# The gate products of a scan-and-feed-forward block are put into silu's pause, and two chunks' finish moves a slot ahead

## Chip, cores and metric

One core of one Trainium2 chip. The metric is the device time in microseconds, the median of several executions. Lower is better.

## What is computed

```python
h = layernorm(x) * (1 + ca) + sa                     # x: 2048 tokens x 256
delta = softplus(dt @ dt_proj_w + dt_proj_b)         # dt, B, C: parts of h @ x_proj_w
for each token t:                                    # 16 states n for each of the 256 channels
    s[n] = exp(delta_t * A[n]) * s[n] + delta_t * B_t[n] * h_t
    y_t  = sum_n C_t[n] * s[n] + D * h_t
x = x + ga * y
h = layernorm(x) * (1 + cb) + sb
x = x + gb * (((silu(h @ gate_w.T * gate_s)) * (h @ up_w.T * up_s)) @ down_w.T * down_s)   # 704 wide
```

## The kernel before

The 2048 tokens are four chunks of 512; the 256 channels are two halves of 128 partitions. The kernel runs in steps. Step c (0 to 3) scans chunk c, and a step has 16 slots, one for each state n. Beside the scan, step c does the front (names with F: first normalization, projections, softplus, `u`) of chunk c+1 and the feed-forward part (names with K) of chunk c-1, whose last tasks run over into step c+1. Step 4 is the tail: the feed-forward part of chunk 3, with nothing to scan.

In a slot n of a scanning step:

- ScalarE (ACT) makes `decay` for each half, an exp of 512 columns (line 830). The ring of decays has two buffers, so the decay of a scan can start only when the scan two before it has ended (line 829).
- GpSimd (POOL) makes the drive `u*B[n]` for both halves three slots ahead (line 642).
- VectorE (DVE) runs the two scans s n.0 and s n.1 (line 995).
- The product `C[n]*state` is made one slot later (`KEEP_LAG`), by POOL for the n in `POOL_C` (line 654), else by DVE (line 969). For DVE's, TensorE (PE) first spreads row n of C over the partitions into the one bank `rows_ps` (line 1294). This row matmul waits until the last DVE product has read the bank.
- PE adds each product into `sums` three slots later, by eight 128x128 transposes (line 1320); the last three of a chunk come together in slot 0 of the next step.

The side tasks stand in tables by hand, `PLAN` and its special cases, as (slot, task) for each engine; an engine runs its slots strictly in order. Slot 12 is after the first half's scan or decay, 12.5 after the second half's. Slots of 16 and over lie in the next step (17 is slot 1). The K tasks in order: `x2` (DVE, line 895, adds `sums` to the residual when all 16 adds are done), `st0 st1 agg` (statistics), `rstd` (ACT) and `nmr` (POOL, line 617), `xn0 xn1` (ACT, line 713), `h2T` (PE transposes), `hi0 hi1` (ACT, line 745) and `lo0 lo1` (DVE, line 933), `gate0..4` and `mixed` (PE products, line 1241, then an ACT eviction each, line 799), `up0..4` (PE), `silu` (ACT, line 818: an activation table load, the silu of the five gates in one instruction, the silu of the sixth, half gate, and a table load back), `hdn5` (line 942) and `hdn0..4` (line 953) on DVE, which multiply silu's result by the up products, `down0..3` (PE, lines 1273 and 1274, each a block of 128 tokens; they wait for hdn5 and hdn4), and `out0 out1` (DVE, line 960), each for two downs. PE has three side banks; `PLACE` gives each product its bank, and a product waits until the user before has emptied it. `rows_ps` and the two decay banks count as banks 3 to 5.

The front's tasks on the same engines include `xT` (PE), `hmod0 hmod1` (ACT, line 728), `z` (PE, line 1193), `abs`, `zb`, `exp`, `ln` (ACT), `bc` (PE, line 1193, and ACT), `clo` (DVE, line 901), `delta0 delta1` (DVE, line 909).

Chunk 0's downs and outs stand in `SPREAD`, chunk 1's in `LATER`, chunk 2's whole K part in `CLOSING`, chunk 3's in `FINAL`. The end of the scanning is thus: last scan of step 3, product 15, its add, `x2` of chunk 3, then the tail.

Of the kernel before, what the change touches and what calls it, by code (L numbers as in the profile page):

```python
# [43 lines left out]
POOL_C = [[4, 6, 9, 11, 13]] + [[1, 3, 5, 7, 9, 11, 13]] * (NCH - 3) + [[1, 3, 5, 6, 7, 10, 13]] + [[1, 2, 4, 5, 7, 8, 10, 12, 13, 14]]  # L44
# [39 lines left out]
SECOND_LATER = {"st0": -7, "st1": -7, "agg": -7}  # L84
# [27 lines left out]
        (19, "K out0"), (22, "K out1"),  # L112
# [1280 lines left out]
```

## Time and profile before

| what | us |
|---|---|
| median of three runs | 315.76 (315.1 to 317.17) |
| the profiled execution, its own time | 314.61 |
| its span in the trace | 312.8 |
| DVE busy in the span | 256.8 (82%) |
| PE busy | 248.9 (80%) |
| POOL busy | 227.0 (73%) |
| ACT busy | 183.7 (59%) |

The span is the time from the first to the last instruction in the trace; the execution's own time lies 1.81 us above it. Matmul time is modelled in part, so a busy PE is not a PE at its peak. The mean granted TensorE clock was 0.874 of the full one.

### The profile page before, as it was taken

Reading aid. Unit: us, or ns where it says so; the run is one execution under the profiler, and the core shown is the slowest. Engines: PE = TensorE matmul, PEld = TensorE weight load, DVE = VectorE, ACT = ScalarE, POOL = GpSimd, SP = SyncE. Lnnn points to the kernel's source line nnn. Section 1 sums busy time; section 2 is a strip of 40 time slices with the busy share of each in tenths; the row PEclk is TensorE's granted clock in tenths of the full one; section 3 lists DMA queues with packets and bytes.
Section 4 is the critical chain, followed back from the end, with each engine's and each line's share of the span. In section 5 each row is a group of like instructions: output and inputs, shape, how many; then the busy total and the mean of one; then the engine's idle time right before and its main releaser. Section 6 shows DMA issues by size and latency. Waiting matters only on the chain. (4 is left out here: it accounts for less than half of the span.)

```text
span 312.8 us, 3793 instructions
## 1 busy us (share of the span) xinstructions
PE 248.9 (80%) x1226; PEld 185.5 (59%) x1226; DVE 256.8 (82%) x330; ACT 183.7 (59%) x294; POOL 227.0 (73%) x113
## 2 busy tenths in 40 slices
PE   7876799846387787848889997667899947897995
PEld 7634796435274455635658675446687835685874
DVE  3589966999999899969999999599988959944420
ACT  2688544765845976896349867932464883306400
POOL 1007789999999999979879997995599996700000
PEclk9995559997579889965999999958799995999999
DMA  7916897469262743392524735725636400001002
GB/s 249 327 48 162 156 143 203 69 104 233 73 133 72 137 103 107 72 147 28 124 69 108 161 90 118 135 38 151 167 90 149 118 1 0 2 0 67 2 0 71
DMA packets 33173, 33.09 MB, mean 106 GB/s; under 512 B 14912, under 2 KB 20224, under 8 KB 33152
## 3 DMA queue, kind: packets, MB, share of 16 engines
q1 hardware_dynamic: 32736, 32.01, 44.7%
q10 hardware_dynamic: 416, 0.81, 0.8%
q8 instruction: 12, 0.20, 0.3%
q14 instruction: 9, 0.07, 0.1%
HBM read 30.40 MB, written 2.36 MB: 105 GB/s over the span
## 5 line engine op out<-in xcount | busy, mean ns | idle before, releaser
L642 POOL TENSOR_TENSOR drv<-u,brow 128x1024 f32<-128x1024 f32 x63 | 147.8, 2362 | 21.0 <-DVE u L917 17.1
L830 ACT ACTIVATE decay<-delta,A 128x512 f32<-128x512 f32 x128 | 87.6, 688 | 82.9 <-DVE state L995 81.0
L995 DVE TENSOR_TENSOR_SCAN state<-decay,last,drv 128x512 f32<-128x512 f32 x96 | 119.1, 1268 | 11.7 <-ACT decay L830 11.4
L654 POOL TENSOR_TENSOR drv<-state,crow 128x1024 f32<-128x1024 f32 x29 | 68.7, 2369 | 9.9 <-DVE state L995 9.9
L1320 PE MATMUL sums<-ident,drv 128*128 128x128 f32 x512 | 72.1, 294 | 0.7 <-POOL drv L654 0.5
L1320 PEld LDWEIGHTS sums<-ident,drv 128*128 128x128 f32 x512 | 62.6, 151 | 12.0 <-issue 7.8
L969 DVE TENSOR_TENSOR drv<-state,rows_ps 128x1024 f32<-128x1024 f32 x35 | 41.8, 1195 | 5.4 <-PE rows_ps L1294 5.4
L1241 PE MATMUL side<-h_hi,ffn_hi 128*128 128x512 f32 x76 | 30.0, 479 | 18.6 <-DVE gates L942 16.1
L995 DVE TENSOR_TENSOR_SCAN state<-decay,drv 128x512 f32<-128x512 f32 x32 | 37.5, 1207 | 1.7 <-issue 1.1
L1294 PE MATMUL rows_ps<-c_parts,sel 64*128 64x512 f32 x35 | 19.6, 561 | 22.9 <-DVE drv L969 22.9
L1273 PE MATMUL side<-down_sb,gates 128*128 128x256 f32 x120 | 30.4, 403 | 4.3 <-DVE gates L953 3.5
L1273 PEld LDWEIGHTS side<-down_sb,gates 128*128 128x128 f32 x120 | 22.9, 199 | 10.3 <-issue 7.4
L1241 PEld LDWEIGHTS side<-h_hi,ffn_hi 128*128 128x128 f32 x76 | 14.5, 220 | 24.5 <-issue 23.0
L1241 PE MATMUL side<-h_lo,ffn_hi 128*128 128x512 f32 x76 | 26.5, 433 | 0.0
L1294 PEld LDWEIGHTS rows_ps<-c_parts,sel 64*128 64x128 f32 x35 | 7.2, 206 | 32.5 <-DVE drv L969 27.9
L1241 PEld LDWEIGHTS side<-h_lo,ffn_hi 128*128 128x128 f32 x76 | 16.4, 216 | 4.3
L799 ACT ACTIVATE gates<-side,wb,pack_sb 128x512 f32<-128x512 f32 x18 | 13.6, 768 | 3.3 <-PE side L1241 3.2
L1193 PE MATMUL side<-hmod,W_sb 128*128 128x512 f32 x24 | 11.0, 603 | 3.7 <-ACT hmod L728 3.7
L953 DVE SCALAR_TENSOR_TENSOR gates<-side,wb,gates 128x512 f32<-128x512 f32 x17 | 12.4, 736 | 1.5 <-PE side L1241 1.5
L1257 PE MATMUL decay<-down_sb,gates 128*128 128x256 f32 (+1 forms) x48 | 11.2, 387 | 0.0
L617 POOL TENSOR_TENSOR nmr_K<-negmean_K,rstd_K 128x4 f32<-128x4 f32 x4 | 0.8, 199 | 13.6 <-ACT rstd_K L706 13.6
L1306 PEld LDWEIGHTS sums<-diag_D,hmod 128*128 128x128 f32 x64 | 9.2, 225 | 1.7 <-issue 1.7
(142 smaller groups left out, 291.9 us busy)
## 6 DMA issues: line engine op xcount, KB each, us to landing
brow<-bc_dram SPq DMA_DIRECT2D x31, 512.0 KB, 5.5
crow<-bc_dram SPq DMA_DIRECT2D x13, 512.0 KB, 7.0
resid<-in_x SPq DMA_DIRECT2D x4, 512.0 KB, 5.4
out<-resid SPq DMA_DIRECT2D x8, 256.0 KB, 2.2
gates<-in_wmod ACTq DMA_DIRECT2D x1, 768.0 KB, 6.1
gates<-in_wmod SPq DMA_DIRECT2D x1, 768.0 KB, 8.7
last<-state SPq DMA_DIRECT2D x48, 1.0 KB, 2.5
crow<-bc_dram SPq DMA_DIRECT2D x3, 256.0 KB, 3.7
```

The source lines that it names most:

```text
L642: nc.gpsimd.tensor_tensor(drv[j % RING_DRV][:, :, 0:S], u[:, c % 2, :, 0:S], b.unsqueeze(1).to_broadcast([P, HALVES, S]), ALU.mult).then_i ...
L654: nc.gpsimd.tensor_tensor(drv[j % RING_DRV][:, :, 0:S], state[j % RING_STATE][:, :, 0:S], row.unsqueeze(1).to_broadcast([P, HALVES, S]), A ...
L799: nc.scalar.activation(gates[:, j, 0:S], src[:, 0:S], ACT.Silu if c == NCH - 1 else ACT.Identity, bias=wb[:, j:j + 1], scale=pack_sb[:, CO ...
L830: nc.scalar.activation(decay[i % RING_DECAY][:, 0:S], delta[:, c % 2, h, 0:S], ACT.Exp, scale=A[:, h * N + n:h * N + n + 1]).then_inc(deca ...
L953: nc.vector.scalar_tensor_tensor(gates[:, j, 0:S], src[:, 0:S], wb[:, FULL + j:FULL + j + 1], gates[:, j, 0:S], ALU.add, ALU.mult).then_in ...
L969: nc.vector.tensor_tensor(drv[j % RING_DRV][:, :, 0:S], state[j % RING_STATE][:, :, 0:S], rows_ps[:, 0:S].unsqueeze(1).to_broadcast([P, HA ...
L995: nc.vector.tensor_tensor_scan(state[j % RING_STATE][:, h, 0:S], decay[i % RING_DECAY][:, 0:S], drv[j % RING_DRV][:, h, 0:S], before, ALU. ...
L1241: ins = nc.tensor.matmul(to[:, 0:S], weights, data, start=part is h2_hi and k == 0, stop=part is h2_lo and k == HALVES - 1)
L1257: ins = nc.tensor.matmul(to[:, b * D:(b + 1) * D], gates[part, j, rows], down_sb[part, j, :], start=j == FULL and b == 0, stop=j == FULL - ...
L1273: nc.tensor.matmul(to, gates[:, j, rows], down_sb[:, j, :], start=j == 0, stop=False)
L1294: nc.tensor.matmul(rows_ps[:, 0:S], sel[:, n:n + 1].to_broadcast([2 * 2 * N, P]), c_parts[:, c % 2, 0:S], start=True, stop=True).then_inc( ...
L1320: ins = nc.tensor.matmul(sums[:, b * D + h * P:b * D + (h + 1) * P], of[:, h, b * P:(b + 1) * P], ident[:, :], is_transpose=True, start=Fa ...
```

## The change

The products of the two slots before silu leave their places and stand behind the two scans of silu's slot: in steps 1 and 2 products 10 and 11 come after scans 12.0 and 12.5, in step 3 products 8 and 9 after scans 10.0 and 10.5 (`SILU_SLOT`, `product_slot`, `row_slot`). For that POOL takes other products, as many as before in every step. From K nmr and xn on, the K tasks of chunks 0 and 1 stand about a slot earlier, silu at 12.5 and not 13.5, hdn0 to hdn4 one to two and a half slots earlier, downs and outs of these chunks one slot earlier; in `CLOSING` hdn1 to hdn3 stand up to 1.5 slots earlier. The half gate's silu runs first and has a semaphore of its own, so hdn5 waits for it alone. Three up products change banks, one into `rows_ps`. In step 3 the row matmul of product 15 stands in slot 13 and no longer after the adds of slot 15. F agg, rstd and nmr of chunk 1 move from ahead of the first scan into slots 0.5 and 1 of step 0, and F exp1 of each chunk moves by half a slot.

```diff
-POOL_C = [[4, 6, 9, 11, 13]] + [[1, 3, 5, 7, 9, 11, 13]] * (NCH - 3) + [[1, 3, 5, 6, 7, 10, 13]] + [[1, 2, 4, 5, 7, 8, 10, 12, 13, 14]]
+POOL_C = [[4, 6, 9, 11, 13]] + [[1, 3, 5, 7, 9, 12, 14]] * (NCH - 3) + [[1, 3, 5, 6, 7, 12, 14]] + [[1, 2, 4, 5, 7, 10, 11, 12, 13, 14]]
+SILU_SLOT = [None, 12, 12, 10]
...
-        (17.5, "K hdn4"), (1.5, "K x2"), ..., (19, "K out0"), (21, "K out1"),
-        (7.5, "K lo0"), (8, "K lo1"), (8, "F clo"), (9.5, "F delta0"), (10.5, "F delta1"),
+        (1.5, "K x2"), ..., (19, "K out0"), (21, "K out1"),
+        (6.5, "K lo0"), (7, "K lo1"), (8, "F clo"), (9.5, "F delta0"), (10.5, "F delta1"),
-        (14.5, "K hdn5"), (15, "K hdn1"), (15.5, "K hdn0"), (16.5, "K hdn2"), (17, "K hdn3"),
+        (12.5, "K hdn5"), (12.5, "K hdn0"), (12.5, "K hdn1"), (14, "K hdn2"), (14.5, "K hdn3"), (15.5, "K hdn4"),
-        (11, "F u"), (-2, "F nmr"), (4, "K nmr"),
+        (11, "F u"), (-2, "F nmr"), (3, "K nmr"),
-        (4.5, "F abs0"), (4.5, "F zb0"), (5, "F abs1"), (5, "F zb1"), (5, "K xn0"), (5.5, "K xn1"), (6, "F exp0"),
-        (6.5, "F exp1"), (7, "K hi0"), (7.5, "K hi1"), (7.5, "F bc"),
-        (7.5, "F chi"), (8.5, "F ln0"), (10, "K gate0"), (10.5, "F ln1"), (10.5, "K gate1"), (11.5, "K gate2"),
-        (12, "K gate3"), (12.5, "K mixed"), (13, "K gate4"), (13.5, "K silu"),
+        (4.5, "F abs0"), (4.5, "F zb0"), (4.5, "K xn0"), (5, "F abs1"), (5, "K xn1"), (5, "F zb1"), (5.5, "F exp0"),
+        (6, "K hi0"), (6.5, "K hi1"), (7, "F exp1"), (7.5, "F bc"),
+        (7.5, "F chi"), (8.5, "F ln0"), (9, "K gate0"), (9.5, "K gate1"), (10, "K gate2"), (10.5, "F ln1"),
+        (11, "K gate3"), (11.5, "K gate4"), (12, "K mixed"), (12.5, "K silu"),
# PLAN, tensor
-        ... (6, "K h2T"), (9, "K gate0"), (9, "K gate1"), (10, "K gate2"), (11, "K gate3"), (11, "K mixed"),
-        (12, "K gate4"), (13, "K up0"), (14, "K up1"), (15, "K up2"), (16, "K up3"), (16, "K up4"),
+        ... (5, "K h2T"), (8, "K gate0"), (8, "K gate1"), (9, "K gate2"), (10, "K gate3"), (10, "K gate4"),
+        (11, "K mixed"), (11, "K up0"), (12, "K up1"), (13, "K up2"), (13, "K up3"), (14, "K up4"),
-SECOND_LATER = {"st0": -7, "st1": -7, "agg": -7}
+SECOND_LATER = {"st0": -7, "st1": -7, "agg": 3, "rstd": 2.5, "nmr": 3}
# LATER: vector, tensor, sync
-        (19, "K out0"), (22, "K out1"),
+        (18, "K out0"), (21, "K out1"),
-        (18, "K down0"), (18, "K down1"), (21, "K down2"), (21, "K down3"),
+        (17, "K down0"), (17, "K down1"), (20, "K down2"), (20, "K down3"),
-        (19, "K out0"), (23, "K out1"),
+        (18, "K out0"), (22, "K out1"),
# CLOSING: vector, tensor
-        (11.5, "K hdn5"), (11.5, "K hdn0"), (12, "K hdn1"), (12.5, "K hdn2"), (13, "K hdn3"), (13, "K hdn4"),
+        (10.5, "K hdn5"), (10.5, "K hdn0"), (10.5, "K hdn1"), (11.5, "K hdn2"), (12, "K hdn3"), (13, "K hdn4"),
-        (9, "K up0"), (10, "K up1"), (12, "K up2"), (12, "K up3"), (12, "K up4"),
+        (9, "K up0"), (10, "K up1"), (11, "K up2"), (11, "K up3"), (12, "K up4"),
# SPREAD: vector, tensor, sync
-        (21.5, "K out0"), (24.5, "K out1"),
+        (20.5, "K out0"), (23.5, "K out1"),
-        (18, "K down0"), (20, "K down1"), (22, "K down2"), (23, "K down3"),
+        (17, "K down0"), (19, "K down1"), (21, "K down2"), (22, "K down3"),
-        (22, "K out0"), (25, "K out1"),
+        (21, "K out0"), (24, "K out1"),
# PLACE, PLACE_CLOSING
-    "K up0": 1, "K up1": 0, "K up2": 2, "K up3": 0, "K up4": 1, "K down": (1, 1),
+    "K up0": 1, "K up1": 0, "K up2": 2, "K up3": 1, "K up4": 0, "K down": (1, 1),
-    "K up0": 0, "K up1": 2, "K up2": 1, "K up3": 0, "K up4": 2, "K down": (1, 2),
+    "K up0": 0, "K up1": 2, "K up2": 3, "K up3": 1, "K up4": 0, "K down": (1, 2),
+LAST_ROW = 13
...
+def product_slot(c, n):
+    if SILU_SLOT[c] is None or n not in (SILU_SLOT[c] - 2, SILU_SLOT[c] - 1):
+        return n + KEEP_LAG
+    return SILU_SLOT[c] + (0 if n == SILU_SLOT[c] - 2 else 0.5)
+
+def row_slot(c, n):
+    if (c, n) == (NCH - 1, N - 1):
+        return LAST_ROW
+    return n + (SILU_SLOT[c] is not None and n == SILU_SLOT[c] - 1)
...
-                    nc.scalar.activation(gates[:, 0:FULL, 0:S], gates[:, 0:FULL, 0:S], ACT.Silu)
                     rest = gates[REST:P, FULL, 0:S]
-                    nc.scalar.activation(rest, rest, ACT.Silu)\
+                    nc.scalar.activation(rest, rest, ACT.Silu).then_inc(silu5_ready, 1)
+                    nc.scalar.activation(gates[:, 0:FULL, 0:S], gates[:, 0:FULL, 0:S], ACT.Silu)\
                       .then_inc(silu_ready, 1)
...
-                        dve.wait_ge(silu_ready, c + 1)
+                        dve.wait_ge(silu5_ready, c + 1)        # in hdn5
...
+                elif i >= SIDE and use[0][0] == "K":
+                    pe.wait_ge(prod_dve, rows_upto(NCH) - 1)   # take(), for up2 in rows_ps
...
+                if (c, n) == (NCH - 1, N - 1):
+                    pe.wait_ge(*emptied(("K up2", NCH - 2, 0)))  # spread_row()
```

## Rows read from the trace of the kernel before

**Rows 1.** Waits of DVE, 84 to 276 us: who waited for whom, total, times, longest

```profile
DVE state L995 <- ACT decay L830: 11.4, 9, 3.6
DVE resid L960 <- PE side L1274: 2.2, 2, 1.4
```

**Rows 2.** Timeline of DVE behind silu in steps 1, 2, 3: start, us

```profile
138.60 2.46 DVE L995 TENSOR_TENSOR_SCAN state<-decay,last,drv 128x512 f32<-128x512 f32 x2 [2.42 <-ACT decay L830]
...
202.75 2.46 DVE L995 TENSOR_TENSOR_SCAN state<-decay,last,drv 128x512 f32<-128x512 f32 x2 [3.58 <-ACT decay L830]
...
256.44 2.46 DVE L995 TENSOR_TENSOR_SCAN state<-decay,last,drv 128x512 f32<-128x512 f32 x2 [3.37 <-ACT decay L830]
```

**Rows 3.** Timeline of ACT, silu of step 1

```profile
132.29 1.28 ACT L818 ACT_TABLE_LOAD   x1
133.58 2.34 ACT L818 ACTIVATE gates<-gates 128x2560 f32<-128x2560 f32 x1
135.94 0.63 ACT L820 ACTIVATE gates<-gates 64x512 f32<-64x512 f32 x1
136.58 1.28 ACT L822 ACT_TABLE_LOAD   x1
```

**Rows 4.** Groups by line and shape, step 2 (146.6 to 210.8 us): busy us, mean ns

```profile
L995 DVE TENSOR_TENSOR_SCAN state<-decay,last,drv 128x512 f32<-128x512 f32 x32 | 39.9, 1269 | 4.3 <-ACT decay L830 4.3
...
L830 ACT ACTIVATE decay<-delta,A 128x512 f32<-128x512 f32 x33 | 22.6, 688 | 21.3 <-DVE state L995 21.2
...
L969 DVE TENSOR_TENSOR drv<-state,rows_ps 128x1024 f32<-128x1024 f32 x9 | 10.7, 1193 | 0.0
...
L953 DVE SCALAR_TENSOR_TENSOR gates<-side,wb,gates 128x512 f32<-128x512 f32 x6 | 4.4, 732 | 0.0
```

**Rows 5.** Timeline of DVE, step 1: product 15, x2, scan 5.0

```profile
85.45 1.18 DVE L969 TENSOR_TENSOR drv<-state,rows_ps 128x1024 f32<-128x1024 f32 x1
...
91.90 1.22 DVE L895 TENSOR_TENSOR resid<-resid,sums 128x1024 f32<-128x1024 f32 x1 [0.59 <-PE sums L1320]
...
103.29 1.28 DVE L995 TENSOR_TENSOR_SCAN state<-decay,last,drv 128x512 f32<-128x512 f32 x1 [0.27 <-ACT decay L830]
```

**Rows 6.** Timeline of ACT, step 1: xn0 of chunk 0

```profile
104.42 1.09 ACT L713 ACTIVATE xn_K<-resid,nmr_K,rstd_K 128x256 f32<-128x256 f32 x2
```

**Rows 7.** Timeline of PE: row 15 of step 0 after a pause, adds in step 1

```profile
83.22 0.79 PE L1294 MATMUL rows_ps<-c_parts,sel 64*128 64x512 f32 x1 [4.78 <-DVE drv L969]
...
87.48 4.39 PE L1320 MATMUL sums<-ident,drv 128*128 128x128 f32 x24
```

**Rows 8.** Stretches of step 1: length, PE busy, PEclk (granted clock), DMA share, GB/s

```profile
90.00:92.00 2.00, 2.00 (x17) 0.83 0.64 159
112.00:134.00 22.00, 16.62 (x97) 1.00 0.35 86
```

**Rows 9.** Timeline of PE, step 2: F z, and the end of down3

```profile
159.71 3.67 PE L1193 MATMUL side<-hmod,W_sb 128*128 128x512 f32 x8 [0.83 <-ACT hmod L728]
...
180.14 0.70 PE L1274 MATMUL side<-down_sb,gates 64*128 64x256 f32 x2
```

**Rows 10.** Timeline of DVE: out1 of step 2, out0 of step 3, step 3's end

```profile
180.88 0.69 DVE L960 TENSOR_TENSOR resid<-resid,side 128x512 f32<-128x512 f32 x1
...
227.73 0.69 DVE L960 TENSOR_TENSOR resid<-resid,side 128x512 f32<-128x512 f32 x1 [1.38 <-PE side L1274]
...
275.35 1.22 DVE L969 TENSOR_TENSOR drv<-state,rows_ps 128x1024 f32<-128x1024 f32 x1 [1.70 <-PE rows_ps L1294]
278.99 1.22 DVE L895 TENSOR_TENSOR resid<-resid,sums 128x1024 f32<-128x1024 f32 x1 [2.42 <-PE sums L1320]
```

**Rows 11.** Timeline of PE, step 3: down0 of chunk 1, down0 and down1 of chunk 2, last adds

```profile
220.00 4.08 PE L1273 MATMUL side<-down_sb,gates 128*128 128x256 f32 x10 [2.62 <-DVE gates L953]
...
267.86 2.40 PE L1273 MATMUL side<-down_sb,gates 128*128 128x256 f32 x10 [0.83 <-issue]
...
275.24 3.71 PE L1320 MATMUL sums<-ident,drv 128*128 128x128 f32 x32
```

More of the change, by code:

```diff
@@ L65 @@
         (-1.5, "F rstd"), (0, "F xn0"), (0.5, "F xn1"), (2.5, "F hmod0"), (3, "F hmod1"), (3.5, "K rstd"),
[4 rows of a table removed]
[4 rows of a table added]
     ],
     "tensor": [
-        (1, "F xT"), (18, "K down0"), (18, "K down1"), (3, "F z"), (20, "K down2"), (20, "K down3"), (6, "K h2T"),
-        (BC_SLOT, "F bc"), (7, "F sp"), (9, "K gate0"), (9, "K gate1"), (10, "K gate2"), (11, "K gate3"), (11, "K mixed"),
-        (12, "K gate4"), (13, "K up0"), (14, "K up1"), (15, "K up2"), (16, "K up3"), (16, "K up4"),
+        (1, "F xT"), (18, "K down0"), (18, "K down1"), (3, "F z"), (20, "K down2"), (20, "K down3"), (5, "K h2T"),
+        (BC_SLOT, "F bc"), (7, "F sp"), (8, "K gate0"), (8, "K gate1"), (9, "K gate2"), (10, "K gate3"), (10, "K gate4"),
+        (11, "K mixed"), (11, "K up0"), (12, "K up1"), (13, "K up2"), (13, "K up3"), (14, "K up4"),
     ],
@@ L439, in adaln_block @@
         silu_ready = sem("silu_ready")
+        silu5_ready = sem("silu5_ready")
         hdn5_ready = sem("hdn5_ready")
@@ L1094, in _ @@
                             scan(step, n, h)
-                        for c, m in lagged(step, n, KEEP_LAG) if h == 0 else ():
-                            if m in DVE_C[c]:
-                                times_c(c, m)
+                        for c in (step - 1, step):
+                            for m in DVE_C[c] if 0 <= c < NCH else ():
+                                if c * N + product_slot(c, m) == step * N + n + h / 2:
+                                    times_c(c, m)
                         for task in side_tasks("vector", step, n + h / 2):
@@ L1110, in take @@
                     pe.wait_ge(side_free[i], k)
-                if i >= SIDE and use[0][0] == "K":
+                if i >= SIDE and use[0][0] == "K" and use[1] == NCH - 1:
                     pe.wait_ge(scan_done, UNITS * HALVES)
                     pe.wait_ge(prod_dve, rows_upto(NCH))
+                elif i >= SIDE and use[0][0] == "K":
+                    pe.wait_ge(prod_dve, rows_upto(NCH) - 1)
                 return to, side_full[i]
@@ L1326, in run_step @@
                 for n in range(N):
-                    spread = 0 <= step < NCH and n in DVE_C[step]
-                    follows = spread and (n - 1) % N in DVE_C[step - (n == 0)]
-                    if spread and not follows:
-                        spread_row(step, n)
+                    rows = [m for m in DVE_C[step] if row_slot(step, m) == n] if 0 <= step < NCH else []
+                    follows = bool(rows) and (rows[0] != n or (n - 1) % N in DVE_C[step - (n == 0)])
+                    if rows and not follows:
+                        spread_row(step, rows[0])
                     for task in side_tasks("tensor", step, n):
                         side_work(*task, full_weights)
-                    ending = step == NCH - 1 and n == N - 1
-                    if spread and follows and not ending:
-                        spread_row(step, n)
+                    if rows and follows:
+                        spread_row(step, rows[0])
                     for c, m in adds_at(step, n):
                         add_state(c, m)
-                    if ending and follows:
-                        spread_row(step, n)
             run_step(FIRST_F, True)
```

2 rows, old and new, of the table PLAN are left out of this document.

## The prediction

> **What bounds the kernel.** I read the waits of DVE over the scanning steps 1 to 3 first. DVE waits 15.9 us in 192: 11.4 for ACT's decay and 2.2 for downs [rows 1], 1.7 for a row matmul and 0.6 for adds at one place each [rows 10, 5]; otherwise it works, so a scanning step is as long as DVE's work and its few waits. The timeline shows where the decay is late: 2.42, 3.58 and 3.37 us stand behind silu in steps 1, 2 and 3, 9.4 us together [rows 2]. ACT's timeline shows why: silu's block is 1.28+2.34+0.63+1.28 us, 5.6 us from its first table load to the next decay, in which no decay is made [rows 3]. With that decay (0.69, line 830 in [rows 4]) the next scan comes 6.3 us after the block's start. This is what the change is aimed at. PE is the second thing to read: it has no share in the waits before step 3 except 0.6 us, but it stands exactly on the edge in two places. In step 2 it works without a gap from F z at 159.71 to the end of down3 at 180.84 (21.1 us), and out1 starts on DVE at 180.88 [rows 9, 10]. In step 3 out0 waits 1.38 us for the downs [rows 10]. DVE waits 1.70 and 2.42 us for PE at the end of step 3 [rows 10].
>
> **Silu.** Durations, as one follows the other without a gap, are a little below the means of [rows 4]: scan 1.18, product 1.12, hdn 0.65. In step 1 let e be the end of scan 11.5. ACT then makes decay 12.5 (about 0.8 with its semaphore) and starts silu, so decay 13.0 is ready at e+0.8+6.3 = e+7.1. DVE has two scans (2.4), products 10 and 11 (2.2), hdn5 (0.75; its silu, now first, is ready at e+2.7) and hdn0, hdn1 (1.3; silu of the five gates ends at e+5.05, just as DVE gets there): 6.6. About 0.5 to 0.6 us of waiting is left. So +1.8 us (gain) in step 1, +3.0 in step 2. In step 3 silu comes from the same decays, and product 8, hdn5, hdn0, hdn1 (3.2 us) are done within its 3.37 us of waiting; +2.8 there. The row matmul of product 11 stands behind mixed, up0, an add and up1 on PE: at full clock it ends 0.6 us before DVE asks for it. At half clock the same work would take twice as long, about 4 us more, and that is the upper bound of this wait; I take 0.
>
> **ACT ahead of it.** xn0 (1.09 for two, 1.0 net) moves to 4.5 and both xn and zb1 stand before decay 5.5 [rows 6]. Scan 5.0 waits 0.27 already [rows 5], so decay 5.0 comes 1.0 later; exp0 leaves the way of decay 6.0, so 0.5 us remains lost. Bounds: 0 and 1.0. I take -0.5 in steps 1 and 2. K nmr a slot earlier on POOL holds one drive (2.36) back until rstd; drives run three slots ahead and hide it. In step 0 F agg only changes places with work of DVE; the wait of xn0 for the later nmr is caught by the waits for PE in that step: 0, within 0.3 both ways. On the SyncE queue the outputs stand a slot earlier, ahead of loads for drives some slots away: 0.
>
> **The starts of steps 2 and 3.** All hdn are now done before the step ends: 3 x 0.65 = 2 us of DVE work leaves slots 0 and 1, and with it two up products on PE. From the end of product 15, DVE reaches x2 after four scans and product 0, here two half slots each: 3 x 1.18+1.12 = 4.7 us. x2 needs row 0 and three adds, which can't start before product 15. Step 1 has this very order: product 15 ends at 86.63, x2 starts at 91.90, 5.3 us later with 0.59 of waiting, since the 24 transposes took 4.39 us at a clock that was half for most of them [rows 5, 7]. The half clock stood there because PE had been idle 4.78 us before 83.22; it rose at about 90.7 (0.83 is the mean of the stretch 90 to 92), 7.5 us after PE resumed [rows 7, 8]. In the changed steps PE will have been idle some 6 us before product 15 (its ups are done at slot 14), so the half clock is likely. Bounds of the wait: 0 (three adds at full clock take 2.9) and 1.7 (all three at half clock, 5.5, and the row 0.79). I take step 1's 0.6 for both: -0.6 each.
>
> *A rule against this.* The 24 transposes at 87.48 were nearly all that PE did between 87.5 and the clock's rise at 90.7 [rows 7, 8]. The Trainium skill, "TensorE: Matmul & The Clock Gate", Part 4 (PE-mode transpose), says that transposes don't count as activity for the clock; by that rule, the trace disagrees here, for the clock rose while transposes ran. If the rule held in steps 2 and 3, where nothing but row 0 stands before them, the clock would stay low into the downs, which is the slower rival below.
>
> **The finish of chunk 0 in step 2.** Up to x2 the gain is 1.8-0.5-0.6 = 0.7. F z therefore starts 0.7 earlier, at 159.0. PE's chain to the end of down3 is the same 21.1 us less one add (0.93) that now comes behind: down3 ends at 179.2. out1 on DVE now stands ahead of scan 8.0, clo and scan 8.5, 3.0 us of work that it had behind it before. DVE asks for it at 180.9-0.7+0.5-3.0 = 177.7, and waits 1.5 to 1.7 us. This wait is new: PE, not DVE, sets this place. -1.6. Then silu's +3.0. On entering step 3: 0.7-0.5-1.6+3.0 = 1.6.
>
> **The finish of chunk 1 in step 3.** x2 again -0.6. down0 and down1 (3.1 us each) start when the last add ends, which is when x2 starts, and end 6.0 later; DVE reaches out0 after x2, st0 and scan 2.0, 3.0 later: it waits 3.0, against 1.38 before. -1.6. out1's wait of 0.8 (2.2 in [rows 1], less 1.38) goes, but h2T now stands behind down2 and down3 and holds decay 5.5 by 0.5: +0.3. Then 1.6-0.6-1.6+0.3 = -0.3 when silu comes, and +2.8: 2.5 at the last scans.
>
> **The end.** Before, from the start of the downs at 267.86 to x2 at 278.99 PE had two downs, five adds and row 15 [rows 10, 11], 11.1 us; DVE's 1.70 and 2.42 us were PE's. Row 15 goes ahead (0.45). hdn4 keeps its place, five scans before the end, so the downs start 2.5 earlier. POOL's last product ends some 2 to 3 us before its add comes up: no bound. But PE has little to do for 4 us before these downs. In step 3 a pause of 2.62 us gave a down0 of 4.08 where one at full clock has 2.40 [rows 11]. So 0 to 1.7 is lost; I take 0.9, the middle. Gain 2.5+0.4-0.9 = 2.0. The tail behind x2 is untouched.
>
> **Sum.** +1.8+3.0+2.8 (silu), -0.5-0.5 (ACT), -0.6-0.6 (x2), -1.6 (out1), -1.6+0.3 (step 3), +0.4-0.9 (end): 2.0 us. The profiled execution's 314.61 (span 312.8 and 1.81 around it) becomes 312.6. The median of the runs shown is 1.15 higher, so 313.8 is the predicted time, 0.6% below 315.76.
>
> **Rivals.** *The gain arrives.* The clock is up when steps 2 and 3 start and at the last downs. Then x2 doesn't wait (+1.2), out0 of step 3 waits 1.7 and not 3.0 (+1.3), the last downs are fast (+0.9): 3.4 more, 5.4 in all: 310.4. If out1's wait is also smaller than worked out, 309. For it: PE holds the full clock over 112 to 134 us of step 1 though it works only 16.6 of the 22 us [rows 8], and with hdn2 to hdn4 earlier more of it falls ahead of the pause. Against: [rows 7] show the half clock after a pause of 4.78 us, and the pause at the step's end becomes longer.
>
> *Slower: PE's finish runs at half clock.* Place: row 0, three adds, F xT and down0 at the starts of steps 2 and 3. If the clock rises only behind down0, x2 comes 1.1 later than I take it, and in step 2 F z 1.1+1.0 (xT) +1.7 (down0, 4.08 for 2.40) = 3.8 later, which out1 waits out in full, as PE bounds there; in step 3 out0 1.1+1.7 = 2.8 later. 6.6 less than the forecast: 4.6 slower than before, 320.4. It decides when the clock rises more than about 7 us after product 15's end. For it: 7.5 us in [rows 7, 8]. Against: PE is busier from product 15 on than from 83.22. Half of this price leaves 1.3 slower, 317.
>
> *The products don't fit.* The row matmul of product 11 comes late, or the gates do, and silu's waits stay. Then 5 to 6 of the 7.6 us don't come: 319. Against: PE is at full clock in this part of step 1 [rows 8], and ACT waits 21 us in step 2 for DVE's scans between its decays [rows 4], which leaves room.
>
> **Chances.** Forecast 0.50 (311.3 to 316.3), gain arrives 0.27, half clock 0.17, don't fit 0.06. The range takes in both rivals' middles: 309.4 to 318.6. A change of 1% (3.2 us) is about what a measurement of this kernel can tell from none. Faster by over 1% (below 312.6): the second case whole and a sixth of the forecast, 0.36. Slower (above 318.9): half of the last two and a little, 0.15. Within: 0.49.
>
> **What would show it.** Silu: DVE's wait behind silu at 0.5 to 0.6 in all three steps, and the products of rows 10 and 11 within it. ACT: a wait of about 1.2 for decay 5.0. x2 waits for the adds in steps 2 and 3, 0 to 1.7, beside the granted clock there. New waits for line 1274 at out1 in step 2 (1.6) and out0 in step 3 (3.0). No wait of a product for its row at the end. I am wrong if the outs don't wait (the chain in step 2 has slack that I don't see), or if silu's waits stay over 2 us.

## The result, and the profile of the changed kernel

The changed kernel takes 318.70 us (median of 10 runs, 316.77 to 319.96); the kernel before, run beside it, 315.74 (10 runs, 314.75 to 317.32). The ratio is 1.008, with a 95% interval of 1.0048 to 1.0113: 0.8% slower, where the prediction had 313.8 and a range up to 318.6.

| | before | after |
|---|---|---|
| the profiled execution, its own time | 314.61 | 317.35 |
| its span | 312.8 | 315.6 |
| DVE busy | 256.8 | 257.1 |
| PE busy | 248.9 | 250.4 |
| POOL busy | 227.0 | 227.0 |
| ACT busy | 183.7 | 183.0 |
| mean granted clock of PE | 0.874 | 0.854 |

The work is the same. What changed is who waits. The waits of DVE in the changed kernel, 84 to 280 us (who waited for whom, total, times, longest):

```profile
DVE resid L914 <- PE sums L1345: 9.3, 4, 5.7
DVE state L1014 <- ACT decay L849: 4.7, 7, 1.2
DVE resid L979 <- PE side L1297: 4.5, 2, 2.6
DVE drv L988 <- PE rows_ps L1319: 0.2, 1, 0.2
```

The wait for decays, 11.4 in [rows 1], is 4.7: the change does what it was made for. But the waits for adds are 9.3 (the kernel before had 3.0: the 0.59 of [rows 5] and the 2.42 of [rows 10]), and those for downs 4.5 (2.2 in [rows 1]). Up to x2 of the last chunk DVE waits 18.7 us, against 18.3 before. The gain is there, and waits for PE took all of it back.

Where each wait stands is in the timeline of DVE of the changed kernel (start, us, instruction, the idle time before it and who ended it):

```profile
104.38 1.28 DVE L1014 TENSOR_TENSOR_SCAN state<-decay,last,drv 128x512 f32<-128x512 f32 x1 [1.25 <-ACT decay L849]
...
135.62 1.28 DVE L1014 TENSOR_TENSOR_SCAN state<-decay,last,drv 128x512 f32<-128x512 f32 x1 [0.46 <-ACT decay L849]
...
155.93 1.22 DVE L914 TENSOR_TENSOR resid<-resid,sums 128x1024 f32<-128x1024 f32 x1 [1.51 <-PE sums L1345]
...
180.32 0.69 DVE L979 TENSOR_TENSOR resid<-resid,side 128x512 f32<-128x512 f32 x1 [1.89 <-PE side L1297]
...
202.13 3.63 DVE L1014 TENSOR_TENSOR_SCAN state<-decay,last,drv 128x512 f32<-128x512 f32 x3 [0.45 <-ACT decay L849]
...
220.82 1.22 DVE L914 TENSOR_TENSOR resid<-resid,sums 128x1024 f32<-128x1024 f32 x1 [1.47 <-PE sums L1345]
...
226.59 0.69 DVE L979 TENSOR_TENSOR resid<-resid,side 128x512 f32<-128x512 f32 x1 [2.57 <-PE side L1297]
...
250.66 2.66 DVE L1014 TENSOR_TENSOR_SCAN state<-decay,last,drv 128x512 f32<-128x512 f32 x2 [1.07 <-ACT decay L849]
...
279.88 1.22 DVE L914 TENSOR_TENSOR resid<-resid,sums 128x1024 f32<-128x1024 f32 x1 [5.71 <-PE sums L1345]
...
292.24 0.75 DVE L972 SCALAR_TENSOR_TENSOR gates<-decay,wb,gates 128x512 f32<-128x512 f32 x1 [2.88 <-PE decay L1264]
```

The waits behind silu, 2.42 and 3.58 in [rows 2], are 0.46 and 0.45; the third, 3.37, is gone, since the 1.07 at 250.66 is a decay held up by late gates before silu, not by silu. Those gates came late while PE ran at half clock: behind two short pauses (0.87 and 0.80 us) its granted clock is 0.50 over 242 to 244 us, and a pair of gate products takes 1.05 us.

```profile
241.57 1.05 PE L1264 MATMUL side<-h_hi,ffn_hi 128*128 128x512 f32 x2
```

In e1, e2, e4 and e8 to e11 below the same pair, after the same two pauses, takes 0.62 or 0.63, and the 1.07 isn't there; it is in e0, e3 and e5, which have the 1.05. (E6 has the 1.05 too, and a wait of 0.44.)

The row for product 15, 1.70 us late in [rows 10], is waited for no more. Against that stand 1.51 and 1.47 at x2 of steps 2 and 3, 1.89 at out1 and 2.57 at out0, 5.71 at the last x2 (2.42 in [rows 10]), and in the tail 2.88 for the first gates, 1.60 before.

PE's timeline of the changed kernel shows why. At the start of step 2: row 15 and an add, a pause, then the row of product 0 of the new chunk (row 0) and the 24 transposes of three adds. The same row 0 and transposes in step 3; the first down at the end of the scanning; the first gate of the tail.

```profile
141.99 0.78 PE L1319 MATMUL rows_ps<-c_parts,sel 64*128 64x512 f32 x1 [3.33 <-DVE drv L988]
142.70 1.97 PE L1345 MATMUL sums<-ident,drv 128*128 128x128 f32 x8
...
149.89 0.76 PE L1319 MATMUL rows_ps<-c_parts,sel 64*128 64x512 f32 x1 [5.22 <-DVE drv L988]
150.58 5.31 PE L1345 MATMUL sums<-ident,drv 128*128 128x128 f32 x24
...
214.82 0.76 PE L1319 MATMUL rows_ps<-c_parts,sel 64*128 64x512 f32 x1 [6.38 <-DVE drv L988]
215.52 5.27 PE L1345 MATMUL sums<-ident,drv 128*128 128x128 f32 x24
...
267.06 4.61 PE L1296 MATMUL side<-down_sb,gates 128*128 128x256 f32 x10 [3.31 <-DVE gates L972]
...
288.55 1.02 PE L1264 MATMUL rows_ps<-h_hi,ffn_hi 128*128 128x512 f32 x2 [1.49 <-ACT h_hi L764]
```

And the stretches around them (length, PE busy, granted clock, DMA share, GB/s):

```profile
150.00:156.00 6.00, 6.00 (x28) 0.53 0.52 136
156.00:160.00 4.00, 3.55 (x20) 1.00 0.72 133
215.00:221.00 6.00, 6.00 (x27) 0.54 0.62 174
267.00:272.00 5.00, 4.94 (x12) 0.53 0.00 0
288.50:292.00 3.50, 3.45 (x9) 0.54 0.00 0
```

The row from 156 on stands there for contrast. In the other four PE works almost without a gap and DVE waits for it, and the granted clock is half (1.2 GHz) for nearly the whole stretch. Each follows a pause, of 5.22, 6.38, 3.31 and 1.49 us. But it isn't always that pause that brought the clock down: row 15 at 141.99 took 0.78 us, at half clock already before the 5.22 began, and in the tail the clock is still 0.90 over 288 to 289, so that it fell after the gates had begun.

Cut at the starts of the four x2, the two executions compare thus:

| stretch | before | after | gain | forecast |
|---|---|---|---|---|
| start to x2 of chunk 0 | 91.90 | 92.02 | -0.12 | 0 |
| to x2 of chunk 1 | 63.73 | 63.91 | -0.18 | +0.7 |
| to x2 of chunk 2 | 64.14 | 64.89 | -0.75 | +0.3 |
| to x2 of chunk 3 | 59.22 | 59.06 | +0.16 | +1.0 |
| to the end of the last out | 31.24 | 32.61 | -1.37 | 0 |
| to the span's end | 2.57 | 3.11 | -0.54 | 0 |

The last row belongs to this execution and not to the kernel: the second trace of the changed kernel (e0) has 2.59 there.

### The profile page after: what moved, and what is told of

It reads as the page before. It is cut to its first block and busy times, and to the rows that moved or that the text cites. A ratio compares the mean times of both kernels' runs of the same rounds, so it can differ in the third digit from the quotient of the medians.

```text
span 315.6 us, 3794 instructions
## 1 busy us (share of the span) xinstructions
PE 250.4 (79%) x1226; PEld 190.1 (60%) x1226; DVE 257.1 (81%) x330; ACT 183.0 (58%) x294; POOL 227.0 (72%) x113
## 5 line engine op out<-in xcount | busy, mean ns | idle before, releaser
L1345 PE MATMUL sums<-ident,drv 128*128 128x128 f32 x512 | 76.5, 306 | 0.0
L1345 PEld LDWEIGHTS sums<-ident,drv 128*128 128x128 f32 x512 | 67.7, 159 | 10.3 <-issue 8.1
L1264 PE MATMUL side<-h_hi,ffn_hi 128*128 128x512 f32 x74 | 27.5, 455 | 3.5 <-DVE c_parts L920 1.1
L1264 PE MATMUL side<-h_lo,ffn_hi 128*128 128x512 f32 x74 | 25.7, 428 | 0.8 <-DVE h_lo L952 0.8
L1264 PEld LDWEIGHTS side<-h_lo,ffn_hi 128*128 128x128 f32 x74 | 15.4, 208 | 5.1 <-DVE h_lo L952 1.2
L1264 PEld LDWEIGHTS side<-h_hi,ffn_hi 128*128 128x128 f32 x74 | 13.6, 209 | 7.8 <-issue 6.2
L972 DVE SCALAR_TENSOR_TENSOR gates<-side,wb,gates 128x512 f32<-128x512 f32 x16 | 11.5, 737 | 1.6 <-PE side L1264 1.5
L914 DVE TENSOR_TENSOR resid<-resid,sums 128x1024 f32<-128x1024 f32 x4 | 4.9, 1221 | 9.3 <-PE sums L1345 9.3
```

The source lines that it names most:

```text
L972: nc.vector.scalar_tensor_tensor(gates[:, j, 0:S], src[:, 0:S], wb[:, FULL + j:FULL + j + 1], gates[:, j, 0:S], ALU.add, ALU.mult).then_in ...
L1264: ins = nc.tensor.matmul(to[:, 0:S], weights, data, start=part is h2_hi and k == 0, stop=part is h2_lo and k == HALVES - 1)
L1345: ins = nc.tensor.matmul(sums[:, b * D + h * P:b * D + (h + 1) * P], of[:, h, b * P:(b + 1) * P], ident[:, :], is_transpose=True, start=Fa ...
```

## The experiments

They were made against two theories. A: what silu's pause gives is spent on PE, by its half clock after pauses and by downs that are asked for before PE can have them, so a cure of any of these places brings its wait back as time. The rival in several forms: the loss is not there (it is one odd execution, DVE's own order, the moved products), and such a cure brings nothing; the texts name it as they need it. Times compare with the kernel before, run on the same chip in turn. "x2 to x2" is the time from the first x2 to the last in the trace, 187.09 before and 187.86 after; "the tail" is from the last x2 to the end of the last out, 31.24 and 32.61.

**e0_changed.** The changed kernel again, on another chip.

> The changed kernel itself, once more, as the measure for the others and for a second trace. Expected by all theories: ratio 1.005 to 1.011 to the kernel before. Theory A (the waits for PE at the chunks' boundaries are built in): x2 waits about 1.5 us in steps 2 and 3, out1 1.9, out0 2.6, last x2 5 to 6, as in its first trace. Rival R (the half clock falls where it likes, and the first trace drew a bad hand at the end): the last x2 wait and the tail behind it, 34.0 us from the last x2 to the last out against 31.2 before, differ by over 1 us between the two traces.

Measured: 319.19 (316.83 to 319.96) against 316.43, ratio 1.0066 [1.0026, 1.0105]; x2 to x2 187.98, tail 32.63. Its waits are those of the first trace: x2 1.58 and 1.51, out1 1.89, out0 2.57, the last x2 5.73, the first gate of the tail 2.86. So these belong to the kernel, not to one execution. (The 34.0 of the expectation is 32.61 in the first trace.)

**e1_outs_back.** Out1 of chunk 0 and out0 of chunk 1 back where they stood, a slot later; the downs stay a slot ahead.

```diff
# SPREAD: vector, sync
-        (20.5, "K out0"), (23.5, "K out1"),
+        (20.5, "K out0"), (24.5, "K out1"),
-        (21, "K out0"), (24, "K out1"),
+        (21, "K out0"), (25, "K out1"),
# LATER: vector, sync
-        (18, "K out0"), (21, "K out1"),
+        (19, "K out0"), (21, "K out1"),
-        (18, "K out0"), (22, "K out1"),
+        (19, "K out0"), (22, "K out1"),
```

> The changed kernel with out1 of chunk 0 and out0 of chunk 1 put back by a slot (24.5 and 19; their stores with them), the downs left ahead. Theory A (DVE stands idle at these two for PE's downs): the waits of 1.9 and 2.6 go to under 0.5 each, 3 to 4 us less than the changed kernel; a part (0.6) of the first comes back as a wait for decay 8.0, which stands behind the eviction of F bc. Rival B (PE's own chain to the end of the scanning is the bound, DVE only waits at another place): the last x2 wait of 5.7 grows by what goes here, and under 1 us is gained.

Measured: 315.68 (313.22 to 318.67), ratio 0.9971 [0.9934, 1.0007]; x2 to x2 184.43, 3.4 less than in the changed kernel. DVE's timeline of this kernel, at the two places and behind them:

```profile
178.84 1.28 DVE L1014 TENSOR_TENSOR_SCAN state<-decay,last,drv 128x512 f32<-128x512 f32 x1 [0.64 <-ACT decay L849]
...
218.29 1.22 DVE L914 TENSOR_TENSOR resid<-resid,sums 128x1024 f32<-128x1024 f32 x1 [0.38 <-PE sums L1345]
...
232.69 0.69 DVE L979 TENSOR_TENSOR resid<-resid,side 128x512 f32<-128x512 f32 x1 [1.37 <-PE side L1297]
234.64 1.28 DVE L1014 TENSOR_TENSOR_SCAN state<-decay,last,drv 128x512 f32<-128x512 f32 x1 [1.26 <-ACT decay L849]
```

Out1 and out0 don't wait any more: with one or two scans between, PE is done. But of 1.89 a 0.64 came back at 178.84, and of 2.57 all of it, as the 1.37 and the 1.26. So the outs' own waits are 1.2 of the 3.4 us. The other 2.2 are PE's clock. X2 of step 3 waited 0.38 and not 1.47, since its 24 transposes took 4.18 us and not 5.27: the granted clock is 0.56 over 216 to 217 us and 1.00 behind, so it rose some 3.5 us after row 0, where it took 5.7 in the changed kernel (0.73 over 220 to 221). And the 1.07 before silu is gone. The 3 to 4 us that A named came, two thirds of them by a way that it didn't name. E9 and e11, which have the same outs, show both again (x2 waits 0.51 and 0.49, no 1.07), so they go with the edit; why the clock rises earlier there stays open.

**e2_filler.** Idle products on PE (their result is read by nobody) behind the last slot of steps 1 and 2, in the pause before row 0.

```diff
+            FILLER = {1: 11, 2: 16}
...
+            def filler(step, full_weights):
+                pe.wait_ge(*emptied(("K up3", step - 1, 0)))
+                for _ in range(FILLER[step]):
...
+                        nc.tensor.matmul(side[1][:, 0:512], ffn_hi[:, 0, 0:P], h2_hi[:, 0, 0:512],
+                                         start=True, stop=True)
...
                         add_state(c, m)
+                    if n == N - 1 and step in FILLER:
+                        filler(step, full_weights)
```

> The changed kernel with idle PE work added: 11 (step 1) and 16 (step 2) products of 512 columns into a free side bank at the end of slot 15, read by nobody. Theory A (x2 waits because row 0 and the three adds run at half clock after a pause of 5.2 and 6.4 us): the 24 adds take 2.9 to 3.5 us and not 5.3, the two x2 waits of 1.5 go to 0 to 0.3, downs follow earlier, 2 to 4 us are gained in all. Rival C (the adds are slow because they wait for data, or the clock doesn't rise on this work): adds stay at 5.3 us and the time rises by 0 to 1 us.

Measured: 314.21 (313.25 to 315.90), ratio 0.993 [0.9895, 0.9966]; x2 to x2 184.36. PE's timeline of this kernel, step 2:

```profile
144.74 3.32 PE L1359 MATMUL side<-h_hi,ffn_hi 128*128 128x512 f32 x11
150.14 0.47 PE L1319 MATMUL rows_ps<-c_parts,sel 64*128 64x512 f32 x1 [2.09 <-DVE drv L988]
150.54 2.84 PE L1345 MATMUL sums<-ident,drv 128*128 128x128 f32 x24
...
158.65 5.37 PE L1216 MATMUL side<-hmod,W_sb 128*128 128x512 f32 x8 [1.61 <-ACT hmod L747]
```

The transposes take 2.84 us, not 5.31, and neither x2 waits. That settles the cause of those waits. But of the 1.59 us won up to x2 of chunk 1 nothing was left at out1 of step 2, 88.37 us after the first x2 where the changed kernel has 88.30: F z, after a pause of 1.61 us, met the half clock itself, 5.37 for the 3.67 of [rows 9], and passed it on to the out0, a row and out1 (waits of 1.16, 1.40 and 2.09). What stood at x2 of chunk 2 was the second x2's own 1.5 us. From there to the last x2 2.0 us more were won: out0 waits 1.43 for 2.57, and the 1.07 before silu is gone.

**e3_close_downs.** The closing down0 and down1 and the hdn4 that they wait for a slot and half a slot earlier.

```diff
# CLOSING: vector, tensor
-        ... (12, "K hdn3"), (13, "K hdn4"),
+        ... (12, "K hdn3"), (12.5, "K hdn4"),
-        (14, "K down0"), (14, "K down1"), (17, "K down2"), (17, "K down3"),
+        (13, "K down0"), (13, "K down1"), (17, "K down2"), (17, "K down3"),
```

> The changed kernel with hdn4 of chunk 2 at 12.5 and not 13, and its down0 and down1 in slot 13 and not 14. Theory A (the last x2 waits 5.7 us because PE starts two downs of 3 to 5.3 us only 5 scans before the end): downs start 2.4 us earlier, at about 4.0 us behind row 15, the last x2 comes 2 to 3.5 us earlier. Rival D (the wait is one for POOL's last products, which end at 273.4): last x2 moves by under 1 us.

Measured: 319.53 (317.61 to 322.51), ratio 1.0079 [1.0039, 1.0119]; x2 to x2 190.07, 2.2 more than the changed kernel. A miss, and of the edit's making: in slot 13 row 15 is issued behind the side tasks, so it now stood behind both downs. DVE's and then PE's timeline of this kernel:

```profile
279.23 1.22 DVE L988 TENSOR_TENSOR drv<-state,rows_ps 128x1024 f32<-128x1024 f32 x1 [3.65 <-PE rows_ps L1319]
```

```profile
268.62 4.60 PE L1296 MATMUL side<-down_sb,gates 128*128 128x256 f32 x10 [4.19 <-DVE gates L972]
...
274.30 4.24 PE L1296 MATMUL side<-down_sb,gates 128*128 128x256 f32 x10
```

Product 15 waited 3.65 us for its row and x2 then 4.13. Both downs ran at half clock as well, 4.60 and 4.24, where in the changed kernel only the first did. How much of the 2.2 us is row 15's place and how much the second down's clock isn't divided here, and the run says nothing on earlier downs by themselves.

**e4_products_back.** The products of steps 1 and 2 where they were before (and POOL's share with them); the K tasks stay a slot ahead.

```diff
-POOL_C = ... [[1, 3, 5, 7, 9, 12, 14]] * (NCH - 3) + [[1, 3, 5, 6, 7, 12, 14]] + ...
+POOL_C = ... [[1, 3, 5, 7, 9, 11, 13]] * (NCH - 3) + [[1, 3, 5, 6, 7, 10, 13]] + ...
-SILU_SLOT = [None, 12, 12, 10]
+SILU_SLOT = [None, None, None, 10]
```

> The changed kernel with the products of steps 1 and 2 at their old places (one slot behind their scan, POOL's choice as before); everything else of the change stays, silu at 12.5 too. Theory A (the two products are what fills silu's pause): DVE's waits for a decay behind silu rise from 0.46 and 0.45 to 1.6 to 2.7 us in steps 1 and 2, 2 to 4 us slower than the changed kernel over the two steps at the end of step 2. Rival E (the pause is filled by the earlier hdn, the products bring nothing): both waits stay under 1 us.

Measured: 318.92 (316.96 to 319.78), ratio 1.0083 [1.0055, 1.011]; x2 to x2 188.14, only 0.28 more than the changed kernel. DVE's and then PE's timeline of this kernel, silu's pause of step 1 and the start of step 2:

```profile
134.45 0.76 DVE L961 SCALAR_TENSOR_TENSOR gates<-side,wb,gates 64x512 f32<-64x512 f32 x1 [0.35 <-ACT gates L838]
...
136.82 1.41 DVE L972 SCALAR_TENSOR_TENSOR gates<-side,wb,gates 128x512 f32<-128x512 f32 x2 [1.61 <-ACT gates L839]
...
138.82 1.28 DVE L1014 TENSOR_TENSOR_SCAN state<-decay,last,drv 128x512 f32<-128x512 f32 x1 [0.60 <-ACT decay L849]
...
159.38 1.22 DVE L914 TENSOR_TENSOR resid<-resid,sums 128x1024 f32<-128x1024 f32 x1 [0.63 <-PE sums L1345]
```

```profile
149.99 0.79 PE L1319 MATMUL rows_ps<-c_parts,sel 64*128 64x512 f32 x1 [6.20 <-DVE drv L988]
...
154.22 0.76 PE L1319 MATMUL rows_ps<-c_parts,sel 64*128 64x512 f32 x1 [1.54 <-DVE drv L988]
154.91 4.43 PE L1345 MATMUL sums<-ident,drv 128*128 128x128 f32 x24
```

The products do fill the pause: without them it has 2.56 us of waiting, with them 0.46, and in step 2 it is 1.60 against 0.45. But x2 then waits 0.63 and 0.46 instead of 1.51 and 1.47. That is row 15's doing: with POOL's share as before, DVE makes product 14 again, row 15 must wait for it (149.99), and it and an add stand between PE's pause and row 0 (154.22), so that the clock rises inside the transposes. Of the 3.2 us that the products gain in the two pauses, x2's waits take 1.9 back; at x2 of chunk 2 this kernel is 1.35 behind the changed one, below the 2 to 4 that A named. The 1.07 of step 3 is gone here too, and so 0.28 is left at the last x2.

**e5_close_fill.** Twelve idle products in slot 13 of step 3, ahead of the closing downs; as in e2 otherwise.

```diff
+            FILLER = {3: 12}
...
+                    if n == N - 3 and step in FILLER:
+                        filler(step, full_weights)
```

> The changed kernel with 12 idle products of 512 columns on PE behind add 10 in slot 13 of step 3, ahead of the last chunk's downs. Theory A (the last x2 waits 5.7 us because these downs start at half clock after a pause of 3.3 us): down0 takes 2.4 us and not 4.6, the wait falls to 3.5 to 4, 1.7 to 2.3 us are gained up to the last x2. Rival F (the five adds behind the downs are what lasts): the wait falls by under 0.7.

Measured: 313.87 (313.23 to 316.07), ratio 0.9951 [0.9925, 0.9976]; x2 to x2 185.63, tail 31.24. PE's timeline of this kernel:

```profile
264.14 3.06 PE L1359 MATMUL side<-h_hi,ffn_hi 128*128 128x512 f32 x12 [0.26 <-DVE gates L972]
267.19 2.40 PE L1296 MATMUL side<-down_sb,gates 128*128 128x256 f32 x10
```

The first down is back at 2.40, the last x2 waits 3.44 and comes 2.2 us earlier: the price of the half clock there, to the tenth. The tail is at full clock here, 31.24, though no instruction of it was touched; more on that at the end.

**e6_plan_part and e7_closing_part.** The change divided. e6 has that of steps 1 and 2 alone (step 3's products, `CLOSING`, its banks and row 15 as before); e7 that of step 3 alone.

```diff
# e6, against the changed kernel
-SILU_SLOT = [None, 12, 12, 10]
+SILU_SLOT = [None, 12, 12, None]
-LAST_ROW = 13
+LAST_ROW = 15
...
# e7, against the changed kernel: PLAN, LATER, SPREAD, PLACE, SECOND_LATER as before, and
-SILU_SLOT = [None, 12, 12, 10]
+SILU_SLOT = [None, None, None, 10]
```

> The kernel before with the change in steps 1 and 2 alone (front and K tasks, products 10 and 11, downs and outs a slot ahead, banks of PLACE), step 3's own part (CLOSING, its banks, POOL's choice in step 3, row 15) as before. Theory A (the finish of chunks 0 and 1 costs more than silu's pause gives): the last x2 of a profiled execution comes 0 to 3 us later than in the kernel before, with the waits of 1.5, 1.9, 1.5 and 2.6 as in the changed kernel. Rival G (step 3's own part is what made it slower): 1 to 3 us faster than before.

> The kernel before with the change in step 3 alone: products 8 and 9 behind the scans of silu's slot, hdn earlier, up2 in rows_ps, POOL's choice in step 3, row 15 in slot 13. Theory A: silu's wait of step 3 falls from 3.4 to 0.5 to 1.5, of which the half clock of the last downs takes back about 2: last x2 0 to 2.5 us earlier than before. Rival G: it comes later than before.

Measured: e6 318.09 (316.78 to 321.50), ratio 1.0083 [1.0051, 1.0114], x2 to x2 188.96, tail 31.23. e7 315.64 (314.23 to 318.29), ratio 0.999 [0.9958, 1.0022], x2 to x2 184.98, tail 32.62. So the part in steps 1 and 2 costs 1.87 at the last x2, and step 3's gives 2.11, of which its tail, at half clock, takes 1.38 back. Together they would give 0.24; the whole change has a loss of 0.77, so 1.0 is lost where they meet. The waits that are longer in the whole change are the last x2's, 5.71 for e7's 5.13 (the first closing down takes 4.61 for 4.08), and that for the decay before silu in step 3, 1.07 for e6's 0.44. The last x2 of e6, then of e7:

```profile
281.19 1.22 DVE L914 TENSOR_TENSOR resid<-resid,sums 128x1024 f32<-128x1024 f32 x1 [2.42 <-PE sums L1345]
```

```profile
278.68 1.22 DVE L914 TENSOR_TENSOR resid<-resid,sums 128x1024 f32<-128x1024 f32 x1 [5.13 <-PE sums L1345]
```

**e8, e9, e10: the cures together.** All three have the outs of e1 and the closing idle products of e5. e8 has those of e2 behind steps 1 and 2 as well, e10 behind step 2 only.

```diff
+            FILLER = {1: 11, 2: 16, 3: 12}     # e8;  e9: {3: 12};  e10: {2: 16, 3: 12}
...
+                    if n == (N - 3 if step == 3 else N - 1) and step in FILLER:
```

> The changed kernel with three edits together: chunk 0's out1 and chunk 1's out0 a slot later, idle products behind the last slot of steps 1 and 2 (11 and 16), and twelve in slot 13 of step 3. Theory A (the loss is PE's: its half clock after pauses, and its finish on the edge where the outs ask for it): each edit takes away a wait of its own, so from the median of the changed kernel, 319, the outs take 3.5, the closing idle products 3.7 (2.2 before the last x2, 1.4 in the tail), and those of steps 1 and 2 up to 3 (two x2 waits of 1.5), of which some 1 to 2 comes back because F z of chunk 2 meets the half clock: 310 to 311, ratio 0.98 to 0.985. From the first to the last x2 181 (187.1 in the kernel before). Theory B (DVE's own work sets the time and PE's waits change places): the gains do not add up; 313 to 314, no better than the best of the three alone.

> As above without the idle products of steps 1 and 2: x2 still waits about 1.5 in step 2 and 0.4 in step 3. Theory A: 319 less 3.5 less 3.7: 311.8, ratio 0.987; from the first to the last x2 182.2. Theory B: 313 to 314.

> The outs a slot later, idle products behind step 2 and in slot 13 of step 3, none behind step 1, so that F z of chunk 2 is not touched. Theory A: where step 2's F z at half clock is what gave back the gain of the idle products behind step 1, this is the same as the run with all of them or better, 310 to 311.5; x2 of step 3 without a wait. If the idle products behind step 1 are a gain of their own once out1 asks later, this one is 1 to 1.5 slower than the run with all. Theory B: 313 to 314.

| | median | ratio to before | x2 to x2 | tail |
|---|---|---|---|---|
| e8 | 312.54 (310.59 to 313.78) | 0.9856 [0.9807, 0.9905] | 181.72 | 32.47 |
| e9 | 311.20 (310.06 to 314.53) | 0.9825 [0.978, 0.987] | 182.50 | 31.23 |
| e10 | 311.47 (310.87 to 315.71) | 0.9838 [0.9793, 0.9884] | 181.72 | 32.46 |

The gains add up, as A has it: 5.4 us less than in the changed kernel between the x2 of e9, where e1 and e5 alone had 3.4 and 2.2. The three medians can't be told apart, and e8's lies above the 310 to 311 that A named. The idle products behind step 1 bring nothing at the end (e8 and e10 are equal from x2 to x2): what they win, 62.31 for 63.97 up to x2 of chunk 1, F z gives back, 63.81 for 62.14 to the next. PE's timeline of e8 at that F z:

```profile
160.31 5.37 PE L1216 MATMUL side<-hmod,W_sb 128*128 128x512 f32 x8 [1.61 <-ACT hmod L747]
```

e9 is the simplest of the three, 1.7% faster than the kernel before. E2 and e5, one cure each, are below that kernel as well, by 0.7% and 0.5%.

**e11_tail_fill.** e9 with five more idle products in the tail, between h2T and the first gate (with a matrix of weights as their data).

```diff
-            FILLER = {3: 12}
+            FILLER = {3: 12, 4: 5}
...                                  # another bank and ffn_hi as data
-                    if n == (N - 3 if step == 3 else N - 1) and step in FILLER:
+                    if n == (N - 3 if step == 3 else 3) and step in FILLER:
```

> The changed kernel with the outs a slot later, twelve idle products in slot 13 of step 3, and five more in the tail, between the transposes of chunk 3's h2T and its first gate, where PE waits 1.49 us for ACT. The tail from the last x2 to the last out took 31.2 us where the first gates ran at full clock (0.73 for the first pair) and 32.6 where they ran at half clock (1.02 to 1.22), after the same instructions and the same pause of 1.49. Theory C (the pause lets the clock fall, depending on when it comes): with the pause filled, the first pair takes 0.6 to 0.73, DVE waits 1.6 and not 2.9 for it, the tail takes 31.2 in every run: median 0 to 1.4 below that of the run without these five (311.2), 310 to 311. Theory D (the clock falls for another reason): the first pair may take 1.0 or more all the same, the five idle products in part too, and the median stays at 311 to 312.

Measured: 311.59 (310.28 to 314.75), ratio 0.9882 [0.9836, 0.9928]; x2 to x2 182.44, tail 31.23. PE's timeline of this kernel:

```profile
283.13 1.41 PE L1359 MATMUL side<-ffn_hi 128*128 128x512 f32 x5
284.86 0.73 PE L1264 MATMUL rows_ps<-h_hi,ffn_hi 128*128 128x512 f32 x2 [0.32 <-ACT h_hi L764]
```

The gates run at full clock, but they did so in e9's trace too, without the five, and the median is not lower. One trace agrees with C, the median lies in D's range, and no run decides between them; this stays open.

## Why the prediction was wrong, step by step

**Silu: right.** Waits of 0.5 to 0.6 were forecast behind silu; 0.46 and 0.45 stand there, and none in step 3. The rival that the products don't fit falls. What the sum didn't have is the 1.07 before silu in step 3.

**ACT ahead of it: right.** A wait of 1.2 for decay 5.0 was forecast; it is 1.25 in step 1 (and 0.67 in step 2).

**"I take step 1's 0.6 for both": wrong.** The waits at x2 are 1.51 and 1.47, near the upper bound of 1.7 that stood beside it. Step 1 was taken as the pattern ("this very order"), but the order isn't the same. There DVE makes product 14 of the chunk, row 15 has to wait for it, and PE resumes with row 15 and an add at 83.22, ahead of product 15. The clock rose 7.5 us after that, in the middle of the transposes: 4.39 us. PE's timeline of the kernel before, behind row 15 in [rows 7]:

```profile
83.94 1.97 PE L1320 MATMUL sums<-ident,drv 128*128 128x128 f32 x8
86.78 0.76 PE L1294 MATMUL rows_ps<-c_parts,sel 64*128 64x512 f32 x1 [0.87 <-DVE drv L969]
```

The change gave product 14 of steps 1 and 2 to POOL, and with it row 15 moved in these steps too, not in step 3 alone. So row 15 and its add were done before the pause (141.99), and row 0 at 149.89 is the first thing behind it; row 0 and nearly all 24 transposes ran at half clock, 5.31, and the clock rose some 5.8 us after row 0 (0.66 over 155 to 156). The wait of step 1 holds only for the order of work of step 1. This is 0.9 in each of two stretches. E2 shows the clock's part by taking it away, and e4, with POOL's share as before, has row 15 and an add behind the pause again and waits of 0.63 and 0.46, the forecast 0.6.

**The finish of chunk 0: right, but a little short.** out1 waits 1.89 where 1.5 to 1.7 were forecast. **The finish of chunk 1:** out0 waits 2.57 for 3.0, and from x2 of chunk 2 to the end of the last scan DVE gained 1.85 us (52.03 for 53.88), where -1.6, +0.3 and +2.8 make 1.5.

**"So 0 to 1.7 is lost; I take 0.9, the middle": wrong.** The first down took 4.61 after a pause of 3.31 us; the 4.08 of [rows 11] stood after one of 2.62 us. 2.2 lost instead of 0.9; e5 gives just 2.2 back. With 0.4 for row 15 the end loses 1.8, and 1.7 is what the traces show (1.85 at the scans, 0.16 at x2). The longer pause was foreseen; its price was averaged with that of a full clock, which no row showed after such a pause.

**"The tail behind x2 is untouched": wrong in the time.** Its instructions are untouched, but its first gates ran at half clock in both traces of the changed kernel, and the tail took 32.61 for 31.24. That the change causes this isn't shown: e3, e5 and e6 have 31.2.

The forecast of the ledger was a gain of 2.0 in the span, the result a loss of 2.8. Of the 4.8 between, 1.8 lie at the x2, 1.3 at the closing down, 1.4 in the tail and 0.5 behind the last out (in the first trace alone); that is 5.0, and small differences of both signs (out1 0.3 worse, the scans of step 3 0.35 better) are the rest. The rival of PE's half clock had the mechanism, and the median, 318.7, lies between its half price, 317, and its whole one, 320.4. That it does is in part luck, for it put the price on F z and down0 behind the adds, and none on the closing down and the tail. F z and down0 ran at full clock (2.32 for down0 at 156.60), since the clock rose just at the end of the adds.

**The rule against this.** In the changed kernel all that PE did from 149.89 to 156.60 was one row matmul and 32 transposes, and in the stretch from 156 on the clock is 1.00. The clock rose while transposes ran. The Trainium skill, "TensorE: Matmul & The Clock Gate", Part 4 (PE-mode transpose), says that the full clock doesn't engage for them, since they don't count as PE being busy in the same way; by that the downs behind them would have run at half clock. The traces disagree in steps 1 to 3, and the measurement decides.

## What to carry to other kernels

When work is moved ahead on an engine that feeds another, look at the pause that it leaves behind: here hdn2 to hdn4 and two up products, taken out of the next step's start, left PE idle for 5 to 6 us just before work that DVE waits for, and what the order gave was lost again on waits for PE, in good part by its half clock. Small work placed behind such a pause counts too: giving one product to POOL let row 15 slip ahead of the pause, and cost about 0.9 us at each x2. A consumer needn't be moved ahead by as much as its producer: leaving the outs where they were was worth 3.4 us here, 1.2 by their own waits and the rest by the clock that PE then had. And cut traces at marks that both kernels have before comparing them, so that a stretch that the edit doesn't touch can't speak in the total.

## What was not expected of the hardware

Idle products on PE are a cure with a price of its own place: eleven of them halved the time of 24 transposes (5.31 to 2.84), twelve that of a down (4.61 to 2.40), and yet those behind step 1 gained nothing, because the next pause, of 1.61 us, then met the half clock.

The same instructions after the same pause don't get the same clock. The tail's first gates wait 1.48 or 1.49 us for ACT in every trace but that of e11, after the same downs and transposes at full clock; in the kernel before, e3, e5, e6 and e9 they then ran at full clock (tail 31.2), in the changed kernel, e0, e1, e2, e4, e7, e8 and e10 at half (32.5 to 32.6). The gates of step 3 are a second such place (1.05 or 0.63 a pair, after pauses of 0.87 and 0.80). What decides it stays open.

It is so in the front as well. E1 and e9 have the same code up to the idle products in slot 13 of step 3. The stretch from 10 to 20 us in e1, then in e9:

```profile
10.00:20.00 10.00, 8.13 (x30) 1.00 0.50 183
```

```profile
10.00:20.00 10.00, 9.03 (x25) 0.51 0.52 185
```

With a clock of 1.00 there, the first x2 starts at 91.82; with 0.51 at 96.44. Between them lie e7, e8 and e11 (0.83; 93.70 to 93.93) and e3 and e4 (0.66; 94.52 and 94.25). A difference of 4.6 us between two executions has nothing to do with the edit, and it is more than the whole change. The runs without a trace show only that time and mean clock go together: in the changed kernel from 316.77 us at 0.854 to 319.96 at 0.839, in e9 from 310.06 at 0.878 to 314.53 at 0.858. So the medians of e8 to e11, of six runs each, carry such an uncertainty, and the distances between the x2 are the better measure.
